# Filler products on the matmul engine in the waits of three normalisations, one softmax and a router

## What is computed

```python
x = x + xattn(ctx, ctx, layernorm(x), wi, Wo, bo)      # one 64-wide head, tiled 16 times into Wo
# attention block, on h = layernorm(layernorm(x)); pattention(x, K, V) = softmax(512**-0.5 * x @ K.T) @ V
k, q, v = pattention(h, kK, kV), pattention(h, qK, qV), pattention(h, vK, vV)
o = pattention(causal_sdpa(q, k, v), pK, pV)           # 16 heads of 32
y = o + x_in
x = x + pattention(layernorm(y), fK, fV) + y           # 2048 keys
# experts
scores = layernorm(x) @ gate_w.T                       # top 2 of 8, softmax over the two
y = sum(prob[e] * (silu(h1) * h2) @ w3[e].T)           # h1, h2 = x @ w12[e].T
```

## Time and profile before

| | |
|---|---|
| time, median of 3 runs | 563.63 us (563.63 to 563.70) |
| profiled execution | 565.72 us |
| its span, first to last instruction | 563.9 us |
| PE busy | 505.0 us (90%) |
| DVE busy | 425.0 us (75%) |
| ACT busy | 328.4 us (58%) |
| POOL busy | 36.3 us (6%) |
| mean granted clock of PE | 0.962 |

### The profile page before, as it was taken

How to read it: one execution, slowest core, us unless ns; L and a number is a source line. 1 busy time by engine, 2 the same in 40 slices (tenths; PEclk the granted TensorE clock), 3 DMA queues, 4 the chain that set the end, 5 groups by cost and what they waited for, 6 DMA issues and landing times.

```text
span 563.9 us, 11010 instructions
## 1 busy us (share of the span) xinstructions
PE 505.0 (90%) x4155; PEld 339.4 (60%) x4155; DVE 425.0 (75%) x704; ACT 328.4 (58%) x638; POOL 36.3 (6%) x109
## 2 busy tenths in 40 slices
PE   5989999999999697489988789894899999999995
PEld 1434544445444254178856568674778888888873
DVE  2377777877778876858664766998888998998994
ACT  2444554455544254645655536983687787888772
POOL 3000000000002300000312000001000000000000
PEclk9999999999999797989999889996899999999999
DMA  8899888888888200416420210378677987986001
GB/s 336 309 350 388 335 324 326 326 325 324 320 346 300 76 1 2 149 76 224 150 74 2 79 71 9 141 298 303 226 285 305 359 305 275 391 312 221 1 1 41
DMA packets 35937, 122.45 MB, mean 217 GB/s; under 512 B 2609, under 2 KB 2609, under 8 KB 31282
## 3 DMA queue, kind: packets, MB, share of 16 engines
q1 hardware_dynamic: 35602, 121.27, 57.7%
q10 hardware_dynamic: 288, 0.52, 0.3%
HBM read 121.26 MB, written 0.52 MB: 216 GB/s over the span
## 4 chain that ended last, share of the span: by engine, by line
PE 46%; DVE 9%; ACT 5%; issue 1%; DVEq 0%; POOL 0%; ACTq 0%
PE score_banks L987 15%; PE bank L1020 8%; PE score_banks L657 2%; PE score_banks L844 2%; PE score_banks L704 2%; PE score_banks L947 2%; PE score_banks L868 2%; DVE w_split L1744 1%; PE bank L667 1%; PE bank L844 1%; PE bank L996 1%; PE bank L537 1%; PE bank L657 1%; ACT arena L1303 1%; PE score_banks L667 1%
## 5 line engine op out<-in xcount | busy, mean ns | idle before, releaser
L1068 ACT ACTIVATE xprobs<-score_banks,small 128x512 f32<-128x512 f32 (+1 forms) x104 | 67.9, 664 | 104.3 <-DVEq L1479 69.3
L1604 DVE TENSOR_TENSOR w_split<-arena,w_split 128x1024 fp32r<-128x1024 f32 x96 | 114.2, 1221 | 6.7 <-ACT w_split L1199 4.5
L1199 ACT ACTIVATE w_split<-arena 128x1024 fp32r<-128x1024 f32 x96 | 100.7, 1060 | 14.8 <-PE score_banks L987 10.5
L491 PE MATMUL bank<-arena,wi_sb 128*64 128x512 f32 (+1 forms) x400 | 93.3, 608 | 6.4 <-DMA arena<-in_ctxT 6.4
L987 PE MATMUL score_banks<-w_split,xg 128*128 128x512 f32 x384 | 88.6, 390 | 1.4 <-ACT xg L1367 1.4
L1488 DVE STREAM_TRANSPOSE xprobsT<-xprobs 128x1024 f32<-128x1024 f32 (+1 forms) x52 | 61.6, 1184 | 34.8 <-ACT xprobs L1068 33.5
L987 PEld LDWEIGHTS score_banks<-w_split,xg 128*128 128x128 f32 x384 | 71.8, 188 | 17.0 <-ACT xg L1367 1.7
L1460 DVE TENSOR_REDUCE small<-score_banks 128x2 f32<-128x1024 f32 (+1 forms) x52 | 57.4, 1139 | 16.2 <-PE score_banks L522 16.1
L491 PEld LDWEIGHTS bank<-arena,wi_sb 128*64 128x64 f32 x400 | 27.0, 140 | 56.1 <-issue 54.8
L522 PE MATMUL score_banks<-k_full,hT 64*32 64x256 f32 (+1 forms) x1664 | 51.7, 382 | 9.4 <-ACT xprobs L1068 8.2
L537 PE MATMUL bank<-xprobsT,v_rows 128*64 128x256 f32 x392 | 48.5, 391 | 0.0
(11 more groups left out here) (281 smaller groups left out, 716.6 us busy)
## 6 DMA issues: line engine op xcount, KB each, us to landing
arena<-in_ctxT SPq DMA_DIRECT2D x23, 2048.0 KB, 9.1
arena<-in_w12T SPq DMA_DIRECT2D x32, 1024.0 KB, 6.0
arena<-in_w3T SPq DMA_DIRECT2D x16, 1024.0 KB, 5.7
arena<-in_fKT SPq DMA_DIRECT2D x4, 1024.0 KB, 7.2
arena<-in_fV SPq DMA_DIRECT2D x4, 1024.0 KB, 5.2
arena<-in_ctxT SPq DMA_DIRECT2D x4, 512.0 KB, 6.1
arena<-in_Wo SPq DMA_DIRECT2D x1, 2048.0 KB, 13.3
arena<-in_kKT SPq DMA_DIRECT2D x1, 1024.0 KB, 11.1
```

The source lines that it names most:

```text
L491: last = pe.matmul(kp_bank[b][DH * h:DH * (h + 1), 0:half], wi_sb[:, k, :], ctx_buf[:, b, k, h * half:(h + 1) * half], start=(k == 0), sto ...
L1068: act.activation(xprobs[:, qb, 0:2 * width].rearrange("p (h n) -> p h n", h=2), score_banks[:, 2 * p:2 * p + 2, 256 * q:256 * q + width], ...
L1199: act.activation(w_split[:, i % 4, 0, :], raw, ACT.Copy).then_inc(part_high, 1)
L1604: return dve.tensor_tensor(w_split[:, i % 4, 1, :], raw, w_split[:, i % 4, 0, :].bitcast(F32), ALU.subtract)
```

## The change

A helper `keep_awake(bk, n)` issues n products of `ident_r` and `mask_r`, 128x384, each complete in itself (start and stop), into a bank that no instruction reads before something else starts a new sum there. It is called at ten places in PE's stream, the two in the loop over the e tiles twice: 69 products in all. Ahead of the first group PE waits for the mask (`mask_ready`) and for both halves of the first weight's high part (`attn_high`). Nothing else changes; DVE, ACT, POOL and SP keep their instructions, and later lines move down (657 becomes 663, 667 becomes 673, 844 becomes 858, 888 becomes 904, 947 becomes 965).

```diff
+            def keep_awake(bk, n):
+
+                for _ in range(n):
+                    pe.matmul(bk[:, 0:3 * P], ident_r[:], mask_r[:], start=True, stop=True)
...
             B = SB + [bank[0], bank[1]]
+            pe.wait_ge(ev("mask_ready"), 2)
+            pe.wait_ge(ev("attn_high"), 2)
+            keep_awake(SB[0], 8)
             turn_rows(hln, [T6, T7], "h", [0])
+            keep_awake(SB[0], 6)
...
-            for st in range(ST):
-                turns_of("p", st)
+            keep_awake(SB[0], 4)
+            turns_of("p", 0)
+            keep_awake(SB[0], 4)
+            turns_of("p", 1)
             for st in range(ST):
                 rows_out("p", st, B[3 + st])
+            keep_awake(SB[0], 3)
             turn_rows(hln, [T6, T7], "f", [0])
+            keep_awake(SB[0], 4)
...
             for st in range(ST):
+                keep_awake(bank[0], 4)
                 turn_rows(hln, [T6, T7], "e", [st])
+                keep_awake(bank[0], 4)
...
             pe.wait_ge(ev("logits_taken"), 1)
+            keep_awake(bank[0], 16)
...
             pe.matmul(counts[:, 2, :], ones_r, chosen[:, 1, :], start=False, stop=True).then_inc(ev("counted"), 1)
+            keep_awake(bank[0], 8)
```

## The result

The changed kernel took 560.71 us (median of 6 runs, 559.40 to 561.84) against 563.84 us for the kernel before beside it (median of 6, 563.63 to 565.75). The ratio is 0.9928, interval 0.9914 to 0.9942, that is 4.1 us faster. The two medians alone are 3.1 us apart; the time is spread by more than a microsecond on both sides, and the ratio's interval is 3.3 to 4.8 us. The forecast was 4.2 us. Two executions of the kernel before, of 665 and 1290 us, fell in a slower state of the chip and are in no ratio.

What follows compares the result with a forecast made beforehand. PE's clock falls in its waits, and PE, DVE and ACT bound these places in turn. Gains of 2.65 us at p and f and 1.55 at e, router and gather sum to 4.2 us: 559.4 us, range 556.9 to 562.4.

Steps and rivals of the forecast that it cites:

- What bounds the kernel, and the cost of a lower clock: Later stages wait on PE, DVE and ACT in turn; 13.7 us of clock lost, costing only PE's waited-for extra work.
- What one filler costs: Each of 69 added products takes 0.175 us at full clock, at most 0.35 at the lower; nearly all in waits.
- The h normalisation: 8 + 6 fillers are hidden in PE's waits; the clock still falls, so gain taken as 0, other end 2.1 us.
- the rival, that the clock holds at h: At the h normalisation the clock stays up too, 2.1 us more gain, 557.3 us in all; chance 0.16.
- The p softmax and the f normalisation: 4 + 4 and 3 + 4 fillers stop two clock falls: -1.4 + 0.1 - 1.35 = -2.65 us.
- The e normalisation and the router: Fillers from e to the gather: logits 0.4 us earlier, gather gains 1.15 us, in sum -1.55 us.
- The four fillers without cover: Ahead of the second tile's e transposes, four fillers outlast PE's wait and cost 0.4 us.
- The gather: Its 16 products run at full clock, 1.86 us shorter; DVE's two subtractions, late next, leave 1.15 us.
- The sum and the range: -2.65 - 1.55 = -4.2 us, giving 559.4 us with chance 0.56; range 556.9 to 562.4 us.
- the second rival: Only a part holds: p and f falls stay, or the gather stays slow; 561.0 to 562.1 us, chance 0.15.
- The slower rival: Clock already low when the router's 16 fillers begin: +3.2 us, 566.8 us, or 564.2 with p and f; chance 0.06.
- The change doesn't do what it says: Rival: such fillers, into a bank nobody reads, don't keep the clock anywhere; 563.6 to 564.1 us, chance 0.06.

Runs made afterwards that it cites:

- a1_all: The changed kernel once more, without edit, timed beside the kernel before; ratio 0.9917 to the kernel before.
- d4_router34: The changed kernel with 34 fillers in place of 16 ahead of the count products; 560.89 us, ratio 0.9923 to the kernel before.
- b1_h_long: The changed kernel with 18 and 12 fillers in place of 8 and 6 at the h normalisation; ratio 0.9916 to the kernel before.
- b3_pool_set: The changed kernel with POOL's two subtractions for the rows' low part replaced by memsets; ratio 0.9939 to the kernel before.
- c1_dve_low: The changed kernel with POOL's two subtractions for the rows' low part moved to DVE; ratio 0.9943 to the kernel before.
- a2_pf: The changed kernel with only the p softmax and f normalisation fillers, those of h, e and router taken out; ratio 0.9959 to the kernel before.
- a4_thin: The changed kernel with all 69 fillers at 8 columns in place of 384; ratio 0.9999 to the kernel before.
- a3_router: The changed kernel with only the e normalisation and router fillers, those of h, p and f taken out; ratio 0.9977 to the kernel before.

## Why the prediction was right, point by point

- **What bounds the kernel, and the cost of a lower clock.** Right. The two places where the clock came back held 10.2 of the 13.7 us of lost clock in the earlier trace rows, and the mean clocks say the same: 21.7 us of full clock lost before, 11.4 in a1_all. The time that came back was 4.1 us, PE's waited-for work at the lower clock. The rule of the Trainium skill ("TensorE: Matmul & The Clock Gate", "HAM oscillation — how this bites in real kernels"), half of the throttled time, would make it about 10 us, and does not hold for this kernel.
- **What one filler costs.** Right: two in 0.35 us had given 0.175 us. The 34 of d4_router34 start at 383.01, and the next product stands at 389.04: 0.177 each. The upper bound of 0.35 at the lower clock, which no row had shown, is right too: the six fillers behind the h transposes started 0.35 us apart (234.7 to 236.4). None of the 69 delayed anything but the transposes named. The wait for the first weight's split was free: the fillers start at 229.89, directly behind line 641's four records.
- **The h normalisation.** Taken as 0, measured -0.2 in the profile, and the fall stayed. The reason, too little work of PE ahead of the fall, fits: b1_h_long closes the gap and the clock stays. But the rival, that the clock holds at h, was no matter of either-or. The two profiles of b3_pool_set and c1_dve_low show the same 14 fillers winning 1.8 us.
- **The p softmax and the f normalisation.** -1.4 + 0.1 - 1.35 against -1.6, 0.0 and -1.2. At f PE was held back a little more than the 0.3 us reckoned (line 858's 24 products took 6.17 us, the next tile's 5.73), and the three fillers without full cover cost nothing: line 571 starts at 319.47, 0.2 us late, and DVE's statistic hides it, as was said. a2_pf confirms the part as a whole (2.3 us).
- **The e normalisation and the router.** This is the part with a wrong term. The four fillers without cover cost 0.34 us (0.4 forecast), and the second gate products ran at full clock. But "DVE's chain of small steps, of which the clock changes nothing" left out that the chain's second step was not bound by the logits. It ended with POOL's subtraction. That one waits for ACT's copies of the rows, which stand behind the second tile's transposes, the very products that the uncovered fillers made later: it ended 6.08 us after the first gate product before, and 6.46 after. The logits did come 0.5 us nearer to that product, and it bought nothing: first gate product to counts went from 8.30 to 8.43 us. b3_pool_set shows it. So -1.05 us were measured here and -1.55 forecast. The 1.08 us step stood in the timeline that I had read, six times the 0.18 of its neighbours.
- **The gather.** -1.15 forecast, -1.2 measured, with DVE's two subtractions late next, as told.
- **The sum and the range.** -4.2 against -4.1 us, closer than the terms deserve, and that is luck: the router's missing 0.5 us was made up by 0.15 us more at p and f and by 0.2 us in stretches that were put at 0. Two slips change nothing: the three losses of clock add up to 13.6 us, and the range's upper end lies 0.3 us, not 0.4, beyond the second rival's 562.1. The median lies 1.3 us above the forecast time in absolute terms, since I subtracted from a median of three early runs, 563.63; more runs of the same kernel gave medians of 563.84 to 565.0.
- **The slower rival.** Its condition did not come up: the clock was up when the sixteen began. Its price, +3.2 us at the gather for fillers of 0.35 us, was not tested. d4_router34 shows only the step behind it at full clock: 2.0 us late at the counts are 1.3 at the gather. "The change doesn't do what it says" is excluded by the ratios of the change, 0.9928 and 0.9917; a4_thin shows a filler for which it would have been true.

What stays open is why the clock falls in one execution and holds in another of the same kernel. No run controls it; the spread of mean clocks for one kernel (0.976 to 0.988 for b3_pool_set, a part of it in the first stage) shows only that it varies. So it is also open why a wait of 1.8 us behind the gather kept its clock in the change and lost it in b1_h_long and a3_router.

## What to carry to other kernels

Where the matmul engine's clock falls in its waits, as here, a wait costs twice: once itself, and once in the slower products behind it. Products of 384 columns into a free bank won back the second part. Size each group by its own wait, from the pace of the same product in the trace. Look for the next thin stretch behind every gain: here a gain of 1.8 us was paid back in a wait of 1.8 us that had been harmless before, and came out once that was filled. A second gain, of 1.0 us, did not show in the time of the change either, and showed in the profile once the wait was filled.
And a small step that takes several times its neighbours' time can be waiting for something that another engine holds, as here; find who ends when it ends before counting on an earlier start.

## What the runs showed that I had not expected

- A stretch in which PE's records cover 3.00 of 3 us had a clock of 0.50 (a4_thin), and one with 2.72 us a clock of 1.00 (the change): the same fillers, with 8 columns and with 384.
- With a gain upstream (b1_h_long), and with the h, p and f groups gone (a3_router), the clock fell behind the gather, where it had held in the change, at a cost of 1.6 to 1.7 us. On b1_h_long nine fillers removed the fall from the profile.
- DVE's steps of 0.18 us with two inputs in SBUF took 0.69 to 1.22 us while POOL subtracted, and 0.18 while POOL wrote zeros.
